# Moving the q, k and v biases into the weights' last row, and two changes of which engine or place issues small DMAs, in a macaron transformer block

## What is computed

```python
x = x + 0.5 * _L0_ffn_ref(_layernorm(x), w_switch, b_switch, w1, b1, w2, b2)
x = x + _L0_attn_ref(_layernorm(x), ln1_w, ln1_b, wq, bq, wk, bk, wv, bv, wo, bo, ...)
x = x + 0.5 * _L0_ffn_ref(_layernorm(x), w_switch, b_switch, w1, b1, w2, b2)

def _L0_attn_ref(q_x, ...):
    xn = _ln(q_x, ln1_w, ln1_b)
    q = (xn @ wq + bq).reshape(b, n, H, HD).transpose(0, 2, 1, 3)      # k and v alike
    fq = jax.nn.elu(q) + 1.0
    fk = jax.nn.elu(k) + 1.0
    kv = jnp.einsum('bhnd,bhne->bnde', fk, v)                          # per token, over its 16 heads
    qkv = jnp.einsum('bhnd,bnde->bhne', fq, kv)
    qk = jnp.einsum('bhnd,bnd->bhn', fq, fk.sum(axis=1))
    attn = (qkv / (qk[..., None] + 1e-06)).transpose(0, 2, 1, 3).reshape(b, n, c) @ wo + bo
    x = q_x + attn
    h = jax.nn.gelu(_ln(x, ln2_w, ln2_b) @ fc_w + fc_b, approximate=False)
    return x + (h @ proj_w + proj_b)

def _L0_ffn_ref(...):      # top-1 routing to 8 experts, 256 slots each; tokens past an expert's capacity pass through
    h = relu(einsum('ecd,edh->ech', buf_e, w1) + b1); y = einsum('ech,ehd->ecd', h, w2) + b2
```

## Time and profile before

| | |
|---|---|
| median of 3 runs | 798.11 us (796.53 to 802.32) |
| the profiled execution | 800.9 us, span of its records 799.1 us |
| PE busy | 682.9 us, 85% |
| DVE, ACT, POOL busy | 435.8, 402.0, 325.4 us |
| granted clock of PE, mean; in 240 to 260 us | 0.94; 0.85 of full speed |
| DMA engines' busy share in 200 to 260 us | 0.48 to 0.52 |
| store of q, k, v: issue to landing, median | 2.7 us |
| first such store; values load that waits for it; ACT's relu of tile 1 | 181.67; 185.86; 184.49 us |
| issue of a values load (128x16x16), a key load (16x16x16) | 0.45, 0.52 us |
| busiest stretches of DVE in the first experts | 12.18 of 20 us (80 to 100), 11.28 (100 to 120) |
| POOL waits for hn's statistics | 180.1 us in 32 waits |
| ACT's wait for the copy of kvt at 568.80 | 1.46 us |

### The profile page before, as it was taken

How to read it: one execution, slowest core, us unless ns; L and a number is a source line. 1 busy time by engine, 2 the same in 40 slices (tenths; PEclk the granted TensorE clock), 3 DMA queues, 4 the chain that set the end, 5 groups by cost and what they waited for, 6 DMA issues and landing times. The chain is left out here.

```text
span 799.1 us, 17121 instructions
## 1 busy us (share of the span) xinstructions
PE 682.9 (85%) x6187; PEld 589.0 (74%) x6187; DVE 435.8 (55%) x1214; ACT 402.0 (50%) x805; POOL 325.4 (41%) x480
## 2 busy tenths in 40 slices
PE   7649999965766999999989989999999850999994
PEld 5448989954555888888878878878887740999993
DVE  7854654312566466667757667577565361444330
ACT  5754465302232666666656566657554540444430
POOL 6242553221122343444463645453547375043411
PEclk9769999977998999999999999999999985899997
DMA  8486677114445454544445445444434232365620
GB/s 263 158 268 213 214 238 225 49 46 76 87 89 89 66 90 82 89 80 69 100 74 118 63 101 89 73 86 77 79 61 133 93 109 69 101 206 187 208 81 26
DMA packets 284013, 92.44 MB, mean 116 GB/s; under 512 B 213939, under 2 KB 281648, under 8 KB 283930
## 3 DMA queue, kind: packets, MB, share of 16 engines
q1 hardware_dynamic: 279834, 83.02, 43.5%
q0 software_dynamic: 4096, 8.33, 3.3%
HBM read 61.95 MB, written 29.41 MB: 114 GB/s over the span
## 5 line engine op out<-in xcount | busy, mean ns | idle before, releaser
L1476 PE MATMUL bank<-down_w,hids 128*128 128x256 f32 x768 | 108.8, 287 | 3.2 <-POOL hids L706 3.2
L1476 PE MATMUL bank<-hnts,up_w 128*128 128x512 f32 x384 | 105.6, 411 | 0.0
L1476 PEld LDWEIGHTS bank<-down_w,hids 128*128 128x128 f32 x768 | 98.5, 190 | 6.6 <-POOL hids L706 4.4
L706 POOL TENSOR_TENSOR hids<-hid,hids 128x512 fp32r<-128x512 f32 x64 | 82.8, 1294 | 49.5 <-ACT hids L915 48.7
L697 POOL TENSOR_SCALAR sth<-sth 128x1 f32<-128x1 f32 x32 | 7.2, 225 | 180.1 <-DVE sth L1360 180.1
L1476 PE MATMUL bank<-qkv_w,xnts 128*128 128x256 f32 (+1 forms) x384 | 79.3, 346 | 0.0
L1476 PEld LDWEIGHTS bank<-hnts,up_w 128*128 128x128 f32 x384 | 68.4, 191 | 11.6
L1476 PEld LDWEIGHTS bank<-qkv_w,xnts 128*128 128x128 f32 x384 | 63.8, 196 | 8.9 <-issue 0.2
L912 ACT ACTIVATE hid<-bank,cols 128x512 f32<-128x512 f32 x64 | 44.1, 688 | 47.6 <-PE bank L1476 42.6
L1476 PE MATMUL bank<-bias_rows,ones_two 128*128 128x256 f32 (+1 forms) x160 | 55.2, 361 | 13.8 <-ACT feats L902 7.3
L1476 PE MATMUL bank<-a_w,xa_h 128*128 128x256 f32 x256 | 60.1, 379 | 0.0
(11 more groups left out here) (241 smaller groups left out, 1426.4 us busy)
## 6 DMA issues: line engine op xcount, KB each, us to landing
qkv_rows<-feats SPq DMA_DIRECT2D x32, 384.0 KB, 2.7
a_raw<-in_L_ffn_w_dram SPq DMA_DIRECT2D x32, 256.0 KB
a_w<-in_L_ffn_w_dram SPq DMA_DIRECT2D x32, 256.0 KB
b_raw<-in_L_ffn_w_dram SPq DMA_DIRECT2D x32, 256.0 KB
b_w<-in_L_ffn_w_dram SPq DMA_DIRECT2D x32, 256.0 KB
mid_rows<-x_all SPq DMA_DIRECT2D x8, 512.0 KB
x<-mid_rows SPq DMA_DIRECT2D x32, 128.0 KB, 2.2
values<-qkv_rows SPq DMA_DIRECT2D x32, 128.0 KB
```

The lines of the kernel that those rows point to most:

```text
L706: pool.tensor_tensor(hids[1][u % 3][:], hid[u % 2][:], f32(hids[0][u % 3][:]), ALU.subtract).then_inc(s_hidl, 1)
L1476: return pe.matmul(dst, left, right, start=start, stop=stop, skip_group_check=True)
```

## The change

Three things are changed.

1. *Biases.* In `fold_ln1` (now in unit 4 instead of 5) PE also multiplies the piece of raw weights with a tile `last_row` that is zero but for one row, the scale of the 256th dimension: each of 128 partitions gets the scaled last row of the weights, 768 columns, in banks 6 and 7. DVE scales each chunk and takes that row from all its rows (`s_shifted`), six more operations, one unit ahead of ACT's high part; the chunks start in unit 6 instead of 4 (LATE). The row itself becomes zero, and SP writes the folded biases, high and low, in its place in `qkv_w`. In the middle stage `zn` is normalised in 255 columns and its 256th holds 1. Since a normalised token adds up to zero, the products are the same. The two `add_bias` of `qkv` go.
2. *Loads by ACT.* The loads t = 4 to 7 of the queries of tiles 0 to 6 (HELPED) are issued by ACT behind its copy of v in step n + 3, and four of the eight key loads of tile 0 by ACT in step 3.
3. *Slot stores.* `send` stands behind POOL's first `low_hidden` of the step instead of at its end.

```diff
-        LATE = 4
-
-        LN_OF = {0: 0, 2: 2}
+        LATE = 6
+
+        LN_OF = {2: 2}
...
-        FOLD = 5
+        FOLD = 4
+
+
+        SHIFTED = 3 * KD
+        last_row = small_a[:, 0:4].rearrange("p a t -> p (a t)")
+        shift_of = [bank[6][:, 0:D], bank[6][:, D:2 * D], bank[7][:, 0:D]]
...
-                if u == FOLD + 4:
+                if u == LATE + SHIFTED:
                     sp.wait_ge(s_bias_split, 10)
+                    sp.wait_ge(s_wlow, SHIFTED)
                     for i, part in enumerate(bias_q_parts):
-                        sp.dma_start(f32(bias_rows[i:i + 1, 0:3 * D]).rearrange("o (b d) -> o b d", b=3),
+                        sp.dma_start(f32(qkv_w[i][P - 1:P, KD - 1, :]).rearrange("o (b d) -> o b d", b=3),
...
-                for t in range(8):
-                    sp.dma_start(keys[i][t * HEADS:(t + 1) * HEADS, :, t * HD:(t + 1) * HD],
...
+                for t in range(4 if n == 0 else 8):
+                    issue_keys(sp, n, t)
...
+                for t in range(4 if n < HELPED else 8):
+                    issue_queries(sp, n, t)
...
+                if s == 20:
+                    pool.wait_ge(s_blank, 16)
+                for n in passed_at(s):
+                    send(n)
                 if at(s, 5) is not None:
                     root(sth[(s - 5) % 3], s_sth, s_rsh, s - 5)
...
-                for n in passed_at(s):
-                    send(n)
...
+                if s == 3:
+                    act.wait_ge(s_zeros, 6)
+                    act.wait_ge(s_grid[0], 16)
+                    for t in range(4, 8):
+                        issue_keys(act, 0, t)
...
+                n = at(s, 3)
+                if n is not None and n < HELPED:
+                    act.wait_ge(s_grid[n % 2], 16 * (n // 2 + 1))
+                    if n >= 2:
+                        act.wait_ge(s_st2, n - 1)
+                    for t in range(4, 8):
+                        issue_queries(act, n, t)
...
+                if 0 <= u - LATE + 1 < SHIFTED:
+
+                    i, k, c = chunks[u - LATE + 1]
+                    row = piece_view(i)[:, k, c:c + D]
+                    dve.wait_ge(s_folded, 1)
+                    dve.scalar_tensor_tensor(out=row, in0=row, scalar=ln_column(0, k), in1=shift_of[c // D],
+                                             op0=ALU.mult, op1=ALU.subtract).then_inc(s_shifted, 1)
...
+            dve.memset(zn[:, D - 1:D], 1.0).then_inc(s_zn, 1)
...
-                    dve.tensor_scalar(zn[:], x1[n1 % 8][:], st[:, 6:7], st[:, 9:10], ALU.subtract,
+                    dve.tensor_scalar(zn[:, 0:D - 1], x1[n1 % 8][:, 0:D - 1], st[:, 6:7], st[:, 9:10], ALU.subtract,
...
+                    mm(bank[6][:, 0:2 * D], last_row, piece_view(0)[:, KD - 1, 0:2 * D], True, True)
+                    mm(bank[7][:, 0:D], last_row, piece_view(0)[:, KD - 1, 2 * D:3 * D], True, True)
...
-                    add_bias(dst, bias_rows[:, c0:c0 + w], True)
                     for k in range(KD):
                         last = product(dst, (hi[:, k], lo[:, k]),
-                                       (qkv_w[0][:, k, c0:c0 + w], qkv_w[1][:, k, c0:c0 + w]), False, k == KD - 1)
+                                       (qkv_w[0][:, k, c0:c0 + w], qkv_w[1][:, k, c0:c0 + w]), k == 0, k == KD - 1)
```

More of the change, by code:

```diff
@@ L93, in build @@
         C_LN = C_FCB + KM
-        BO, PB = 3 * D, 4 * D
-        BIASES = 5 + E
-        bias_rows = tile(ctx, "bias_rows", [P, BIASES * D], F32R)
+        BO, PB = 0, D
+        PROJ, BIASES = 3, 5 + E
+        bias_rows = tile(ctx, "bias_rows", [P, (BIASES - PROJ) * D], F32R)
         seen_sum = tile(ctx, "seen_sum", [P, 2, E], BF16)
@@ L136, in build @@
         s_piece = sems("piece_loaded", 4)
+        s_shift, s_shifted = sem("last_row_spread"), sem("qkv_rows_shifted")
         s_whigh = sem("middle_high_made")
@@ L324, in build, with issue_keys, issue_queries @@
         PASSED_IN_STEPS = (NG - 2) * GROUP
+        HELPED = 7
+        def issue_keys(engine, n, t):
+            i, rows = n % 2, slice(n * P, (n + 1) * P)
+            engine.dma_start(keys[i][t * HEADS:(t + 1) * HEADS, :, t * HD:(t + 1) * HD],
+                             qkv_rows[1, rows, :].rearrange(
+                                 "(s t) (h d) -> t h s d", t=8, h=HEADS)[t]).then_inc(s_kvin[i], 16)
+        def issue_queries(engine, n, t):
+            i, rows = n % 2, slice(n * P, (n + 1) * P)
+            engine.dma_start(queries[i][t * HD:(t + 1) * HD, :, t * HEADS:(t + 1) * HEADS],
+                             qkv_rows[0, rows, :].rearrange(
+                                 "(s t) (d h) -> t d s h", t=8, d=HD)[t]).then_inc(s_qin[i], 16)
         def set_of(i, j):
@@ L420, in _ @@
                     for i, part in enumerate(bias_parts):
-                        sp.dma_start(f32(bias_rows[i:i + 1, :]).rearrange("o (b d) -> o b d", b=BIASES),
-                                     f32(part[:])).then_inc(s_bias_rows, 16)
+                        sp.dma_start(f32(bias_rows[i:i + 1, :]).rearrange("o (b d) -> o b d", b=BIASES - PROJ),
+                                     f32(part[PROJ:BIASES, :])).then_inc(s_bias_rows, 16)
                     for c in range(PAIRS):
@@ L481, in load_keys @@
                     "(s t) (g e) -> (t g) s e", t=8, g=HEADS)).then_inc(s_kvin[i], 16)
-                for t in range(8):
-                    sp.dma_start(keys[i][t * HEADS:(t + 1) * HEADS, :, t * HD:(t + 1) * HD],
-                                 qkv_rows[1, rows, :].rearrange(
-                                     "(s t) (h d) -> t h s d", t=8, h=HEADS)[t]).then_inc(s_kvin[i], 16)
+                for t in range(4 if n == 0 else 8):
+                    issue_keys(sp, n, t)
             def load_queries(n):
-                i, rows = n % 2, slice(n * P, (n + 1) * P)
                 if n >= 2:
                     sp.wait_ge(s_st2, n - 1)
[L491 to L494, removed]
+                for t in range(4 if n < HELPED else 8):
+                    issue_queries(sp, n, t)
             def store_x2(g):
@@ L732, in _ @@
                     pass_factors_b(routed(s, 2))
-                if s == 20:
-                    pool.wait_ge(s_blank, 16)
-                for n in passed_at(s):
-                    send(n)
             roots_b(NG - 1)
@@ L868, in middle_weights @@
                     i, k, c = chunks[u - LATE]
-                    act.wait_ge(s_piece[i], 16 * len(pieces[i][2]))
+                    if u < LATE + SHIFTED:
+                        act.wait_ge(s_shifted, u - LATE + 1)
+                    else:
+                        act.wait_ge(s_piece[i], 16 * len(pieces[i][2]))
                     high, given = piece_cut(i, pieces[i][0][0], k, c, False), piece_cut(i, piece_view(i), k, c, True)
@@ L1301, in middle_weights @@
                     dve.wait_ge(s_cols, 1)
+                    dve.tensor_scalar(last_row, ident[:, P - 1:P].broadcast_to([P, P]), ln_column(0, KD - 1), None,
+                                      ALU.mult).then_inc(s_shift, 1)
                     for i in range(3):
@@ L1557, in down @@
                     for s in range(ST):
-                        add_bias(dst[:, s * D:(s + 1) * D], bias_rows[:, (5 + x - ex.first) * D:(6 + x - ex.first) * D], s == 0)
+                        add_bias(dst[:, s * D:(s + 1) * D], bias_rows[:, (2 + x - ex.first) * D:(3 + x - ex.first) * D], s == 0)
                 pe.wait_ge(ex.sem.relu, 2 * (u + 1))
@@ L1776, in _ @@
                     dst = bank[B_TURN]
-                    pe.wait_ge(s_zn, n + 1)
+                    pe.wait_ge(s_zn, n + 2)
                     if turn_free:
```

2 lines of the change are left out of this document (added).

## The result

The changed kernel takes 775.11 us (median of 4 runs, 773.87 to 776.58), the kernel before 799.22 us (4 runs, 796.53 to 802.32): ratio 0.970, 95% interval 0.966 to 0.974. Forecast were 770.1 us, 762 to 786. The profiled execution takes 774.8 us (span 773.1) against 800.9 (span 799.1): 26.0 us less in the span, where I had summed 28.0.

A forecast was written before the change was run, and what follows sets the result against it. SP's DMA issues were taken to bound the ramp and PE the steady part from step 10. 11.0 + 9.6 + 9.5 - 2.1 = 28.0 us off the 798.1 us median gave 770.1 us, range 762 to 786.

The forecast's parts named there:

- part 2: Bias matmuls of q, k, v removed: 0.40 us off each of 24 PE-bound steps (10 to 33), 9.6 us.
- part 3: Slot stores moved to mid-step: ACT's copy of kvt no longer held, 9.5 us, bounds 0 and 11.
- Part 1: Ramp, steps 2 to 9: half the queries' loads of tiles 0 to 6 issued by ACT, shortening SP's step; 11.0 us.
- both limits now lie together, and I take 9.35 us: Ramp step: SP's queue about 9.2 us, PE's chain 9.3, so 9.35 instead of 11.0, seven times: 11.5 us.
- the full clock in the ramp: PE's clock also stays full in the ramp (0.85 in 240 to 260 us before); with the fourth stall gone, 762 us.
- Cover: Steady step: PE reaches its need of ACT's copy of v with 0.47 us in hand, just above the 0.43 removed.
- rival (c): Bias matmuls were hidden: ACT's copy of v sets the step from step 11, their removal gives nothing; 780 us, chance 0.08.
- the 1.46 us of the fourth pair: Stall at the fourth pair of slot stores (568.80 us); its going too would raise the stores' gain to 11 us.
- Rival (b): The stall moves with the stores, delaying ACT's relu and copy of v; their move gives 0 to 2, 779 us; chance 0.15.
- Part 4: First expert stage: cost of two fp32 matmuls (1.4 us) and a wait for weights (0.7 us); -2.1 us, bounds -0.5 and -6.
- (a): Ramp: SP's and ACT's issues exclude each other, so SP's step stays at 11 us; 780 us, chance 0.15.
- (d): Slower: ACT's four issues become the ramp's bound; at 2.5 us per issue about 815 us; chance 0.03.

The follow-up runs named there:

- gap_no_move: filler_gap with the slot stores back at the end of POOL's step; 787.4 us, ratio to before 0.984 (chip E).
- filler_gap: Changed kernel plus dummy matmuls where PE waits in the ramp (24 in step 4, 8 in step 6, 8 each in steps 7 to 9); 770.7 us, ratio 0.964.
- no_bias: Changed kernel with the bias matmuls of q, k, v back, with the old fold and chunks; 781.8 us, ratio to before 0.988 (chip B).
- only_loads: Kernel before with nothing but the loads by ACT; 793.4 us, ratio to before 0.991 (chip D).
- only_bias: Kernel before with nothing but the biases of q, k, v moved into the last row of the weights; 784.6 us, ratio 0.993 (chip C).
- only_move: Kernel before with nothing but the slot stores moved to mid-step; 787.7 us, ratio to before 0.996 (chip C).
- unchanged: Kernel before, as it is, measured and profiled again on chip C; 790.7 us, ratio 0.999.

## Why the prediction was right, and where it was not

The total came within 2 us, 28.0 against 26.0 in the spans, by luck: errors cancel in it. On chip A, with part 2 sized by the two runs that isolate it and part 3 by what is left:

| part | forecast | shown |
|---|---|---|
| 1 and the ramp's share of 2 | 11.0 | 6.1 |
| 2, steady part | 9.6 | 6.8 |
| 3, steady part and behind | 9.5 | 15.9 - 6.8 + 3.6 = 12.7 |
| 4 | -2.1 | 0.4, within scatter |

The split between parts 2 and 3 depends on the order. The two runs that isolate part 2 had no hold. Where there is one, moving the stores last gives 11.0 in the steady part and 4.1 behind (gap_no_move against filler_gap, on E and D).

**Part 1**, mechanism right, size wrong. SP's queue was what held the keys, ACT's issues cost 0.45 us (I took 0.52), they run beside SP's, and ACT's copies weren't late. The step that failed is "both limits now lie together, and I take 9.35 us". I took PE's chain as 10.53 - 0.89 = 9.6 us and part 2 as 0.3 off it. Part 2 does take some 0.2 off, but from a longer chain: with the bias matmuls and ACT's loads the short steps take 9.87 and 9.88 us (no_bias, only_loads), without them 9.64. When the keys come in time, PE still waits 0.21 us at the same place for DVE's att_ (only_loads, 221.11), which is most of the difference. And only some steps reach this floor: PE waits 2.2 or 2.3 us in each, and in three of the five from tile 3 to tile 8 part of its matmuls run at the lower clock. I had put the full clock in the ramp at the edge of my range; its price should have been a term of the sum. It is 3.5 to 4.0 us of the ramp (filler_gap).

**Part 2**, mechanism right. The price was 0.35 us per step instead of 0.40; two of my 24 steps lie outside the steady part as it is cut here; and of its 22 four gain only 0.13 us, because they wait for rb_lg. Cover held: PE comes 0.13 us after ACT's copy, so rival (c) is out, but 0.13 us is all that taking more work off PE between these two could still gain before the copy sets the step.

**Part 3**, right on this chip, and for the reason given: the copies of kvt no longer wait. The three pairs of the steady part gave about what I said (9.1 of 9.5). I missed 3.6 us behind tile 31, where I named only the 1.46 us of the fourth pair as an upper bound; 0.2 to 0.8 of them may be part 2's (no_bias, only_bias), and 1.7 came there without any hold too (only_move). My reading that a schedule like this holds the keys' sum is true of three measurements out of five. On chip C the same edit is worth 3.3 us, and its steady part of that comes from zn on DVE instead. Rival (b) didn't show on any chip.

**Part 4**, the work as forecast, its effect on the time not seen. The row's matmuls cost PE 1.39 us (67.27 to 68.66), as I said, with the fold right behind them; the 0.7 us wait for the weights' piece didn't come. But two waits went. PE's waits in 60 to 162 us of the kernel before (what for, us, times, longest):

```profile
PE bank L1488 <- DVE xa_unit L1090: 1.9, 2, 1.5
```

The window of 100 to 120 us, kernel before (span, then busy us and count of PE, PEld, DVE, ACT, POOL, clock, DMA share, GB/s):

```profile
100.00:120.00 20.00, 18.49 (x122) 17.17 (x121) 11.28 (x25) 12.48 (x29) 11.60 (x12) 1.00 0.72 237
```

The same window, kernel after:

```profile
100.00:120.00 20.00, 20.00 (x133) 18.77 (x132) 12.25 (x28) 11.37 (x26) 12.65 (x13) 1.00 0.88 285
```

After, PE has no wait in 60 to 162 us. Over all traces its waits there are 0 to 1.3 us, 0.2 on average, with the row in the weights and 0.2 to 1.9, 1.3 on average, without. That the later chunks (LATE) are what freed DVE there is argued from the order, not tried. Over all runs the first transpose of zn comes at 174.7 us on average in nine traces with the row in the weights and at 174.6 in five without.

**Rivals (a) and (d)** fell by the issues themselves: four by ACT in 1.8 us, in the middle of SP's. SP's eight key loads took 4.9 us on average in the ramp's steps of after, 4.6 in before and 4.7 in unchanged, so each of them is stretched by some 0.04 us.

## What to carry to other kernels

Where a queue is solid with small DMA issues, give some of them to a second engine that has gaps: here ACT took four of a step's eight query loads at 0.45 us each, and SP's own grew by little. Look next at the chain that the queue was hiding, and don't take its floor from a step in which it still waited. In this ramp PE's waits of 2.2 to 2.3 us were paid for twice, once as waits and once as clock: price the clock as a term, and try matmuls without use in those waits. And a stall seen in one trace, even in every pair in the same form, may belong to the chip or the session: run the unchanged kernel in another one before the stall's whole price is promised.

## What I had not expected of the hardware

The same program takes 791 us in two of five measurements and 799 to 801 us in three. The difference of its steady part (284.8 and 292.5 us) lies in the steps in which POOL issues indirect DMAs beside a sum of 32-column matmuls: there the copy that waits for the sum waits 2.3 to 2.4 us in a pair's first step and some 1.2 us in its second in some measurements and is on time in the others. The steps without stores repeat from A to C to 0.03 us.

Forty useless matmuls of 512 columns made a stage of 90 us 2.0 us shorter, and 56 of them, placed in PE's waits, 3.5 to 4.0.
